# Attention rows reordered query by query, one DMA each way per pack, and all short tiles exchanged through DRAM

## The reference

```
x = x + layernorm(attention(layernorm(x), w_qkv, w_dense))
x = x + layernorm(ffn(layernorm(x)))
attention: 32 query heads of width 128, 8 key/value heads (4 query heads share one), causal mask,
           softmax(q k^T / sqrt(128)) v, then w_dense
ffn:       silu(x w1^T) * (x w3^T), then w2^T, INTER = 1792, activations scaled per 128-column block
```

## Time and profile before

| | us |
|---|---|
| median of 3 runs | 1193.05 (1190.01 to 1194.33) |
| the profiled execution's own time | 1197.52 |
| its span, first to last instruction | 1195.7 |
| PE busy / DVE busy / POOL busy / ACT busy | 1117.8 / 862.6 / 804.1 / 640.3 |
| DMA queue of SP: bytes, share of 16 engines | 215.89 MB, 59.8% |
| mean granted TensorE clock | 0.983 of full |

### The profile page before, as it was taken

How to read it: one execution, slowest core, us unless ns; L and a number is a source line. 1 busy time by engine, 2 the same in 40 slices (tenths; PEclk the granted TensorE clock), 3 DMA queues, 4 the chain that set the end, 5 groups by cost and what they waited for, 6 DMA issues and landing times.

```text
span 1195.7 us, 16875 instructions
## 1 busy us (share of the span) xinstructions
PE 1117.8 (93%) x5218; PEld 928.2 (78%) x5218; DVE 862.6 (72%) x1698; ACT 640.3 (54%) x1237; POOL 804.1 (67%) x836
## 2 busy tenths in 40 slices
PE   8999999999989989989988989988899889999997
PEld 7888888888777767777767777867688768888885
DVE  4544546467788878788888878988667896666666
ACT  6432333258577665766766766755468642222224
POOL 7744457437859769677869579857585676656645
PEclk9999999999999999999999989989999999999999
DMA  6444664447899698797797795895430124333422
GB/s 216 137 179 145 190 211 141 143 139 221 255 270 266 200 286 250 219 301 212 257 280 235 242 286 171 265 304 150 128 98 1 53 56 146 94 116 114 119 66 94
DMA packets 157875, 216.89 MB, mean 181 GB/s; under 512 B 41056, under 2 KB 122592, under 8 KB 152928
## 3 DMA queue, kind: packets, MB, share of 16 engines
q1 hardware_dynamic: 157792, 215.89, 59.8%
HBM read 125.00 MB, written 90.83 MB: 181 GB/s over the span
## 4 chain that ended last, share of the span: by engine, by line
PE 54%; DMA 17%; DVE 13%; issue 5%; POOL 4%; ACT 3%; SPq 3%; DVEq 0%; POOLq 0%; ACTq 0%
PE psS L1586 16%; PE psOY L1586 14%; PE psT L1586 11%; DMA squares_long<-p_scr_long 10%; PE psOY L1719 7%; DMA p_scr_long<-probs_long 6%; PE psOY L1734 5%; DVE pT_lo L1242 4%; SPq L497 2%; DVE squares_long L1329 2%; PE psT L1700 2%; POOL pT_lo L662 1%; DVE probs_long L1310 1%; POOL probs_long L722 1%; DVE y L1387 1%
## 5 line engine op out<-in xcount | busy, mean ns | idle before, releaser
L1586 PE MATMUL psS<-kT_hi,qT_hi 128*128 128x384 f32 (+6 forms) x384 | 140.5, 366 | 40.6 <-DVE negmax L1310 40.3
L1329 DVE STREAM_TRANSPOSE squares_long<-squares_long 128x1792 f32<-128x1792 f32 (+3 forms) x54 | 102.2, 1893 | 62.9 <-DMA squares_long<-p_scr_long 62.9
L1036 ACT ACTIVATE probs_long<-probs_long,negmax 128x896 f32<-128x896 f32 (+9 forms) x124 | 122.4, 989 | 35.9 <-DVE negmax L1310 35.3
L722 POOL TENSOR_SCALAR probs_long<-probs_long,rsum 128x768 f32<-128x768 f32 (+9 forms) x98 | 93.2, 961 | 67.5 <-DVE rsum L1317 67.4
L662 POOL TENSOR_TENSOR pT_lo<-squares_long,pT_hi 128x896 fp32r<-128x896 f32 (+3 forms) x47 | 108.7, 2322 | 42.6 <-ACT pT_hi L1031 42.4
L1586 PE MATMUL psS<-kT_hi,qT_lo 128*128 128x384 f32 (+6 forms) x384 | 134.2, 349 | 0.0
L1586 PE MATMUL psS<-kT_lo,qT_hi 128*128 128x384 f32 (+6 forms) x384 | 134.0, 349 | 0.0
L1586 PEld LDWEIGHTS psS<-kT_hi,qT_hi 128*128 128x128 f32 x384 | 75.6, 197 | 58.1 <-issue 34.0
L1734 PE MATMUL psOY<-wd_hi,oT_hi 128*128 128x512 f32 x256 | 104.9, 410 | 10.1 <-DVE oT_lo L1242 8.7
L1031 ACT CAST pT_hi<-squares_long 128x1792 fp32r<-128x1792 f32 (+3 forms) x54 | 84.9, 1572 | 47.9 <-DVE squares_long L1329 47.6
L1242 DVE TENSOR_TENSOR pT_lo<-squares_long,pT_hi 128x896 fp32r<-128x896 f32 (+4 forms) x47 | 105.3, 2257 | 0.2 <-ACT pT_hi L1031 0.2
(11 more groups left out here) (208 smaller groups left out, 3282.6 us busy)
## 6 DMA issues: line engine op xcount, KB each, us to landing
q_raw<-q_scr SPq DMA_DIRECT2D x64, 256.0 KB, 5.3
p_scr_long<-probs_long SPq DMA_DIRECT2D x14, 896.0 KB, 6.3
squares_long<-p_scr_long SPq DMA_DIRECT2D x56, 224.0 KB, 5.7
p_scr_long<-probs_long SPq DMA_DIRECT2D x12, 1024.0 KB, 5.9
squares_long<-p_scr_long SPq DMA_DIRECT2D x48, 256.0 KB, 7.3
p_scr_long<-probs_long SPq DMA_DIRECT2D x14, 768.0 KB, 4.5
squares_long<-p_scr_long SPq DMA_DIRECT2D x56, 192.0 KB, 4.3
raw<-in_w_qk SPq DMA_DIRECT2D x10, 1024.0 KB, 6.4
```

Of the source, the lines that this page charges most:

```text
L722: nc.gpsimd.tensor_scalar(row, row, rsum[:, column(t, u)], 1.0, ALU.mult, ALU.mult).then_inc(p_ready[lane(t)], 1)
L1036: nc.scalar.activation(row, row, ACT.Exp, bias=negmax[:, column(t, u)], scale=-1.0, accum_out=lsum[:, column(t, u)]).then_inc(e_done[lane( ...
L1329: nc.vector.transpose(rows, rows).then_inc(swap_turned[c], 1)
L1586: last = nc.tensor.matmul(dst, a, b, start=(start and k == 0), stop=(stop and k == len(terms) - 1), skip_group_check=resumed)
```

## The change

- **Query by query.** For exchanged steps the partition order within a unit becomes query-major (partition 4q + head), so that the four rows which one destination partition needs are neighbours in the source. `queries_in` and `queries_of` give the new patterns to `restore_q`; it now reads `q_raw` with heads innermost, that is 4 elements that lie 128 elements (512 bytes) apart. The mask's corner in `band` is built for the new order.
- **One load a pack.** The store splits each row in its four quarters and writes them to four regions of DRAM (128 partitions x 4 pieces). The load is then one DMA: each of 128 partitions reads one contiguous piece.
- **Tiles 0 and 1 exchanged.** `STAYING` is empty: the 14 steps go the DRAM way as one pack of four units each, their lo part made by DVE in one instruction.
- **Own banks.** `lane` is 1 for exchanged short steps: their scores go to the two banks of `psT`, with their own counters. Long steps keep `psS`. `FIRST_TURNS` adds the waits between the first PE transposes, these scores, and the last PE transposes, which share `psT`.
- **New weaves.** All five orders are rewritten. In the steps that stay at the end, tile 0 is turned in two parts, not one.

```diff
-    LOWS = {0: (), 1: (), 2: ...}
+    LOWS = {2: ..., 0: (((0, 1, 2, 3), 0),), 1: (((0, 1, 2, 3), 0),)}
-    STAYING = (0, 1)
-    HEADS = {0: ((0, 1, 2, 3),), 1: ...}
+    STAYING = ()
+    HEADS = {0: ((0, 1), (2, 3)), 1: ...}
     def lane(t):
-        return 0
+        return int(away(t) and not length(t))
+    FIRST_TURNS = sum(item[0] < AWAY[0] for item in TURNS)
...
+        def queries_in(tile, t):
+            if away(t):
+                return tile[:].rearrange("p (u q b) -> p u q b", u=HG, b=HG)
+            return from_units(tile)
+        def queries_of(tile, t):
+            return tile[:].rearrange("p (b u q) -> p u q b", u=HG, b=HG) if away(t) else by_head(tile)
+        def kept(t, k):
+            return p_scr[length(t)][pack_count(t, k) % 2, k, 0:P * len(PACKS[TILES[t]][k]) * (TILES[t] + 1) * P]
...
             def swap_away(t, k):
...
-                sp.dma_start(p_scr[c][count % 2, k, :, 0:rows.shape[1]], rows).then_inc(swap_out[c][k], 16)
+                by_quarter = kept(t, k).rearrange("(b p x) -> p b x", b=HG, p=P)
+                sp.dma_start(by_quarter, rows.rearrange("p (b x) -> p b x", b=HG)).then_inc(swap_out[c][k], 16)
             def swap_back(t, k):
...
-                for b in range(HG):
-                    sp.dma_start(rows[b * SPAN:(b + 1) * SPAN, :].rearrange("q (a x) -> q a x", a=HG),
-                                 p_scr[c][pack_count(t, k) % 2, k, :, b * w:(b + 1) * w].rearrange("(a q) x -> q a x", a=HG)
-                                 ).then_inc(swap_in[c][k], 16)
+                sp.dma_start(rows, kept(t, k).rearrange("(p x) -> p x", p=P)).then_inc(swap_in[c][k], 16)
...
-                nc.scalar.copy(from_units(qT[t % 3][0]), by_head(q_raw[t % 2])).then_inc(q_hi, 1)
+                nc.scalar.copy(queries_in(qT[t % 3][0], t), queries_of(q_raw[t % 2], t)).then_inc(q_hi, 1)
...
             def scores(t, u):
                 if softmax_count(t, u) > 2:
                     pe.wait_ge(s_done[lane(t)], softmax_count(t, u) - 2)
+                elif lane(t):
+                    pe.wait_ge(t_done, FIRST_TURNS)
```

More of the change, by code:

```diff
@@ new lines, in sandwich_kernel @@
+    ACT_WEAVE = ("ppeppeqeeopqrpeeppqpperpqpreeenppeppeqnffqfofeeeehofhreefqeefqfkoqhheoeffneqfqfeknfofheehqfofnqkekeohhno"
+             "rfffrqfkkreeorheeqohfqfffeeeekohhqffoeekffqneffohqhenqeokeffqnkeeohhnfffoeqfekkeeohhfqrofffrrqeekreeohhf"
+             "fqeeffokneeqffnohqheffoeqkkneeqohnhoffffqeekkeeqorrfrqfffhhoeekeeffrqohfhqfeoekfnfeohqheonkqffkeeohqeeno"
+             "hqffffneekkroeeqrhrofhffefekqeeqrohheffoeffnqkeohhfqfeonffqeeknkohqeefhoffqfneerrrkkohreefofhqqffeekeeqo"
+             "hhffeoefkfffenqohqheoffnkeeqknfofhfqeehonefeqkkrorhererohfqfkfeefoeqehoqheekeeeoqhhoeeoppppeqeoppppeeppp"
+             "epeaceepoppipejeqoqppeappqpcepepaeeipcjieoppjeeepopapepcpepiappjeopepcppepipeappoppcjxioxagxcxjgxigaxjgc"
+             "xitgjggxdtttgddtd")
@@ new lines, in sandwich_kernel @@
+    POOL_WEAVE = ("bnqnnnqdnqqnnnndnqrmmrmmqnnnnrllnqnqmmrmnmnllqmmnqmmnqlnmqmmmkqlnldqmmknnmmrrlnnqldmqmmmnnnnlqlmmnmmrrqq"
+             "nqlmmmmqnklndlmmqmmnnknnllrrmqmmmnnqnndlmmlqmmnqmrmnrqlmmnqkqnldlmmmmqnnkqnnrrmmmmllnnqdnnmmqllmmnqrrqml"
+             "mnqmmknlqdlnqmmmmnkndrnnllrqmnnqmmnmnllmmqnmmrrqlnqmqmmmnklqdlnmmmmdknnqlnnrlrmqmmmnqnqnnlmmlnmmmqrmqrnl"
+             "mmnqkmmlqnldnmqmnkdlnnlrmqmrmmnqnnnrllnnnqnrlunuunqnnquuynnnaznnxnnnqyunqnaynnxaxnqnnnynaxynnnnanynnxaxw"
+             "ywagwxgywagxggwgwgg")
@@ L313, in sandwich_kernel @@
         h_scr = nc.dram_tensor("h_scr", [RING, P, CW], F32, kind="Internal").ap()
-        p_scr = [nc.dram_tensor(f"p_scr_{n}", [2, HG // 2, P, 2 * size], F32, kind="Internal").ap()
+        p_scr = [nc.dram_tensor(f"p_scr_{n}", [2, HG // 2, P * 2 * size], F32, kind="Internal").ap()
                  for n, size in (("short", BANK), ("long", S))]
@@ L702, in restore_q @@
                 pool.wait_ge(q_hi, t + 1)
-                hi, lo = (from_units(u) for u in qT[t % 3])
-                low(lo, by_head(q_raw[t % 2]), hi).then_inc(q_lo, 1)
+                hi, lo = (queries_in(u, t) for u in qT[t % 3])
+                low(lo, queries_of(q_raw[t % 2], t), hi).then_inc(q_lo, 1)
             def split_dense(g, h):
@@ L941, in _ @@
                     nc.gpsimd.memset(band[:, HG:, 2 * P - SPAN:2 * P], NEG).then_inc(band_ready, 1)
-                    nc.gpsimd.tensor_scalar(band[:, HG - 1, 2 * P - SPAN:2 * P], mask[:, S - SPAN:S], 1.0, 1.0, ALU.mult,
-                                            ALU.mult).then_inc(band_ready, 1)
+                    corner = band[:, HG - 1, 2 * P - SPAN:2 * P]
+                    nc.gpsimd.affine_select(out=corner, in_=corner, compare_op=ALU.is_ge, fill=NEG, base=0,
+                                            pattern=[[-HG, SPAN]], channel_multiplier=1).then_inc(band_ready, 1)
                 elif kind == "zeros":
@@ L1325, in turn_squares @@
                 c = length(t)
-                dve.wait_ge(swap_in[c][k], 16 * HG * pack_count(t, k))
+                dve.wait_ge(swap_in[c][k], 16 * pack_count(t, k))
                 rows = pack_rows(squares[c], t, k)
@@ L1688, in turn_probs @@
                 turn = TURN[item]
+                if FIRST_TURNS <= turn < FIRST_TURNS + 2 and SOFT[1]:
+                    pe.wait_ge(s_done[1], len(SOFT[1]))
                 if turn >= 2:
```

59 lines of the change are left out of this document (23 added, 36 removed).

## The result

| | before | after |
|---|---|---|
| median of 4 runs, side by side, us | 1193.32 (1190.01 to 1194.33) | 1149.38 (1149.06 to 1152.48) |
| span of the profiled execution, us | 1195.7 | 1150.7 |
| its own time, us | 1197.52 | 1152.48 |
| mean granted clock | 0.983 | 0.991 |

The ratio is 0.9642, 95% interval 0.9617 to 0.9667: 44 us, 3.6% faster. Two further sets of the same kernel on other chips gave 0.9667 [0.9631, 0.9702] and 0.9614 [0.9577, 0.965]. The forecast was 1162 us in a range of 1138 to 1187.

The account below looks back on a forecast made before the run. PE was taken to set the time from 285 to 860 us, with some 75 us lost to waits and clock; -7 - 22 - 12 + 10 = -31 took 1193 to 1162 us, range 1138 to 1187.

Parts of the forecast that it names:

- The loads: Exchange loads, 285 to 860 us: 32-partition destinations hold them to 226 GB/s; one 128-partition load moves 400, 108 us less DMA time.
- The DMA share: DMA engines in the exchange stretch: (472 - 84 + 28) / 544 = 0.76, hidden below PE if the loads speed up.
- PE's own work: PE in the exchange stretch: 84 transposes go, 7.4 us, all of it counted because PE is the bound: -7.
- the clock (-12): PE's clock in the exchange stretch: 17 us lost behind long waits, six of eight places go: -12, bounds 0 and -17.
- The mis-sized term: the waits: PE's waits for `negmax` in the exchange stretch: 22 of 25.7 us in six places go, bounds 0 and 39.3.
- +10: DVE in the exchange stretch: 21 us more work, to 496 us; half charged because its idle time shrinks, bounds 0 and 21.
- banks and faster loads cure the same wait; they don't add: Tile 1's scores behind tile 7's transposes on DVE: both parts cure that one wait, so 22 us was booked once.
- the six places once a head: PE waits for `negmax` between 358 and 788 us, where DVE stands for tile 7's loads: 25.7 us in all.
- no part of the change shortens that: At 816.83 us PE stood 4.17 us behind a 6.21 us DVE subtraction, which was to stay.
- the rival in which DVE becomes the bound: Exchange stretch: DVE's 496 us at 0.88 busy make it last 564 us, -11, 1182 us; chance 0.16.
- Query order: nothing on the path: `restore_q`'s strided query copies on ACT and POOL: POOL taken at 1.4 us each, beside idle time, so no time added.
- Tiles 0 and 1 and the transposes: DVE block transposes 1.23 and 0.68 us, low parts 1.71 and 1.0 us, seven times each; 84 PE transposes go.

Follow-up runs that it names:

- experiments 2 and 9: New kernel with each load cut: 2, into four DMAs of 32 partitions, 1184.02 us; 9, into two DMAs of 64 partitions, 1183.14 us.
- Experiment 1: Kernel before with query-major rows, strided query copies, one store and one load a pack; orders, banks, tiles 0 and 1 as before: 1172.22 us, ratio 0.9791.
- experiment 3: New kernel with the rows, stores, four loads and query copies of before; tiles 0 and 1 exchanged, own banks, new orders: 1183.6 us, ratio 0.988.
- experiment 4: New kernel with both query copies (ACT, POOL) in runs of 32 elements again, outputs wrong: 1142.47 us, ratio 0.9572 beside 0.9667 for the new kernel.
- experiment 8: New kernel with DVE's low parts of exchanged rows written as source times 0, one input instead of two: 1131.63 us, ratio 0.9478 beside 0.9667.

## Why the prediction was right, and where its sizes were off

**The loads: right, cause and size.** One load was to move at 400 GB/s; it moves 433, and the rows of experiments 2 and 9 show the 32- or 64-partition destination as the cause, with long pieces and with two DMAs as with four. DVE's wait was to fall below 25 us: 17.4. The DMA share was forecast at 0.76 and is 0.83. That is 444 us of DMA time where 416 were booked. Experiment 1, without tiles 0 and 1, has 0.72 x 560 = 403 where 388 would have been booked, so about half of the miss lies in the rows themselves and half in the two tiles; loads and stores are not split further. This miss had no effect on the time, as the share is not what decides.

**PE's own work: right.** 84 transposes less (-7) and the clock (-12) were to give -19; PE is busy for 17.5 us less. The clock's loss in the stretch fell from 0.03 x 575 = 17.3 us to 0.01 x 535 = 5.4, the 12 of the forecast, as the long waits behind which the clock dropped from 2.4 to 1.2 GHz went.

**The mis-sized term: the waits.** -22 was booked for `negmax`, bounds 0 and 39.3; 39.3 - 4.5 = 34.8 went (28.6 and 32.9 in the profiles of the two further sets). On the other side +10 was charged for DVE's 21 us of new work; the new wait that stands in its place, on POOL's `pT_lo` (2.7 before, 10.0 now), is 7.3 us more, and PE's other waits cancel within about 1 us. -34.8 + 7.3 = -27.5, the idle time that PE lost, against a forecast of -12. That is the whole distance between -31 and -45.

Two steps of the working lie behind it. First, "banks and faster loads cure the same wait; they don't add" was wrong for the time. Loads alone give 0.9791, all the rest with the loads and copies of before 0.9880 (experiment 3); their product is 0.9673, with some 0.009 on either side, and the new kernel measured 0.9614 to 0.9667. They add, within the intervals. On the `negmax` wait itself they overlap a little: 21.6 us and 19.9 us alone (experiments 1, 3), 34.8 together. I had counted only the six places once a head; the other 14 us of the earlier trace rows, rated as staying, went as well. Second, of the 6.21 us subtraction I wrote "no part of the change shortens that", and this was wrong: DVE's subtractions came to stand otherwise against POOL's, and 11 to 18 us of DVE's time went with it. So DVE stood at 478 us (478 to 480 in the three profiles), not at the 496 that were forecast, and the rival in which DVE becomes the bound lost its ground. Experiments 1, 2 and 3 put this down to the rest of the change and not to the loads; that it is the orders is argued, not shown. From one execution to another the same kernel's 128x896 mean goes from 1958 to 2299 ns.

**The small step that failed: "Query order: nothing on the path".** POOL's subtraction stayed below 2 us, as forecast (1.64, not 1.42), but ACT's copy, which I gave no price at all, went from 0.61 to 1.09 us, and together they cost 11 us (experiment 4). The bounds held for the operation, the cover did not. My reading, not shown: idle time elsewhere in the stretch hides a copy only if it isn't just ahead of another engine's work. Nor was the copy all that POOL got: its busy time rose by 28 us (433 to 461), 12 of it the query subtraction and 13 the scaling of long rows, whose mean for 128x768 went from 950 to 1095 ns; the forecast had 3 us besides the copies. The two rules named there fit thus: the Trainium skill's "SBUF — State Buffer", section "Door 1: The DMA port swizzle", says that each crossing to a new 16-byte line pays, without a figure, and both copies did get slower; the +50% that the Trainium skill's "GPSIMD Engine Reference", section "Performance pitfalls for Q7 kernels", gives for custom kernels came as +16% on this instruction (1416 to 1638 ns). The two errors have opposite signs, so the forecast looks better than its steps, and that is luck: without the copies' price the gain would be some 55 us, not 44.

**Tiles 0 and 1 and the transposes** came as priced: 1.23 us (tile 1) and 0.70 (0.68 was forecast) to turn, 1.72 and 0.93 us for the low parts (1.71 and 1.0). The 84 transposes of PE are gone; the next ones start at 814 us and belong to the steps that stay at the end.

**Left open.** The own banks were not undone alone in the new order: PE's order puts scores ahead that need four pairs of banks, so an older bank would need other orders. So experiment 3 does not split banks, orders and transposes (-7.4 us of PE's work by their count). The cost of DVE and POOL subtracting at the same time is not priced either: experiment 8 changed the operation with it. No variant with the whole computation was faster than the new kernel beyond the intervals.

## What to carry to other kernels

Before pricing a DMA by its bytes and pieces, look at a stretch of full share in which it is alone and ask how many partitions it touches: here the half-rate stretch meant that the destination, not the queue, was the limit, and a layout that lets one DMA touch all 128 partitions was worth small pieces on the other side. An engine that is idle for a seventh or a quarter of the time is no sure cover for a slower step that others wait for; take the slower step's whole price as the upper bound. And where two engines subtract at the same time, the mean duration of an instruction belongs to the order of work as much as to the instruction: read its shortest case beside its mean, since a new order can change it. And when an instruction is swapped to price a contention, compare the shortest cases too: the substitute may be faster by itself, as in experiment 8, and then the time gained is not the contention's.

## What the runs showed of the hardware

- Loads to 32 partitions 225 to 228 GB/s, to 64 partitions 221, to 128 433, all with the DMA engines at a share of 1.03 to 1.08. Four loads of 32 in alternating order went at 246 in such a stretch; against two loads of 64 they took 0.9% off the kernel.
- A copy of 128x512 fp32 on ACT costs 0.61 us in runs of 32 elements and 1.08 to 1.09 with a step on every element, whether the step is on the read (512 bytes) or on the write (16 bytes). POOL's subtraction goes from 1.36 to 1.42 us to 1.62 to 1.64.
- A two-input subtraction of 128x896 on DVE takes 1.08 us alone and 4.31 (before: 6.21) beside POOL's subtractions.
- The one-input multiplication of 128x1024 takes 0.70 us alone, where the subtraction takes 1.2, and 2.82 us beside POOL's subtraction of 2.85: it is faster, but it does not escape POOL.
